# A four-stage ViT tower on one core: norm weight applied where the turned gelu rows leave the bank, projection in two terms, last stage written out in another order

## The chip, the core and the metric

The kernel runs on one NeuronCore of one Trainium2 chip. Its engines have queues of their own and meet through semaphores: TensorE (PE, matmuls, with weight loads shown as PEld), VectorE (DVE), ScalarE (ACT), GpSimd (POOL) and SyncE (SP), which here only issues DMAs. Each engine executes its list strictly in the order in which it is written, so an instruction that waits holds back all that stands behind it on its engine. The metric is the device time of one execution in microseconds (us); lower is better.

## The reference

32 images of 96x96 become 38 rows of 256 values each (36 patches, two tokens). Four blocks follow, each added to its input h: causal attention with rotary positions, a mixture of 8 linear experts, an attention with routed values and a small MLP, and a feed-forward part with ternary weights. The change is about the last:

```python
h = jnp.einsum('btd,hd->bth', x, absmean(W_fc))
h = jax.nn.gelu(h, approximate=False)
h = layernorm(h, ln_w, ln_b)
return jnp.einsum('bth,dh->btd', h, absmean(W_proj))
```

`absmean` makes each weight -1, 0 or 1. The hidden width is 1024. `ln_w` and `ln_b` hold one value for each hidden column.

## The kernel before

**Tiles and stages.** Three images make a tile of 114 rows (R), and there are 11 tiles (T). A tile passes stages a (first attention), c1 (experts), c2 and c3 (second attention and its MLP) and d (the last block). Stages overlap: while tile 7 is in c3, tile 10 may be in c1.

**What sets the order.** Every engine has an order written out by hand, as a list of small steps named by stage and tile, such as `c3_r1(9)` or `d2_proj(0)`. There are three loops: one over stage a; one, `c_step`, in which five tiles are in different parts of c1 to c3; and before the change one over the last stage, `d_step` (L2187 on PE), which runs for i from 4 to 10 with tile i - 3 in the projection and younger tiles in earlier steps. Between the first two loops lies a passage written out step by step (from `scores(7, True)`, L2198), and between the second and the third another (from `c2_x(9)`, L2294).

**Exact products.** A float32 value is split in a high and a low part, both in a narrower format that PE takes at full rate (fp32r). `mm3` (L1806) multiplies two such pairs with three matmuls: high by high, high by low, low by high.

**Stage d, tile by tile.** `d1_x` turns the normalised rows with PE; ACT and DVE take the high and low part out of the bank. `d1_fc` multiplies them by the ternary weights `fct`, four matmuls of 512 columns for each half of the hidden width. `d1_gelu` (ACT, L748) writes each half as 114x512 to `gel`; `d2_stats` (DVE, L1424) takes mean and variance of it. `d2_turn` (PE, L2175) turns the eight chunks of 128 columns into two banks, four chunks to a bank. `d2_hi` (ACT, L757) and `d2_lo` (DVE, L1438) write high and low part to `gth` and `gtl`, one instruction of 128x456 for each bank. `d2_proj` (PE, L2178) multiplies by the projection, eight chunks with `mm3`. `d2_centre` (DVE, L1446) subtracts the mean times the column sums `ncs`, `d2_out` (DVE, L1452) scales by 1/std and adds to h, and SP writes the tile out. Since mean and 1/std are applied behind the projection, the norm costs no pass over the hidden rows. There is one buffer each for `gel`, the banks of the turned rows, `gth`/`gtl`, and the projection's bank.

**The norm weight.** It is multiplied into the projection weights: ACT makes a high and a low version of the eight 128x256 chunks (`proj_hi` L726, `proj_lo` L734, 16 instructions), since the product with a float weight isn't ternary any more. `proj_sums` (L2141) sums them with 16 matmuls, `proj_bias` (L2134) adds `ln_b` through eight matmuls in float32, which the profile shows as 16.

Of the kernel before, what the change touches and what calls it, by code (L numbers as in the profile page):

```python
# [33 lines left out]
R = G * S  # L34
# [85 lines left out]
def vit_tower(nc, x_tiles, consts, vectors, rows, w_a, w_c, wqv, w_in, w_out, fc, proj, lnw, out):  # L120
    with ExitStack() as ctx:
# [3 lines left out]
        def sems(names):  # L125
# [42 lines left out]
        ones_r = sb("ones_r", [P, R], F32R)  # L168
# [11 lines left out]
        lnw_c = sb("lnw_c", [P, 2 * HC])  # L180
        lnwc_h = sb("lnwc_h", [P, HC], F32R)
# [13 lines left out]
        lnwc, lnwc_l = (lnw_c[:, i * HC:(i + 1) * HC] for i in range(2))  # L195
        lnbr = k_exp[:].rearrange("p f h r -> p (f h r)").rearrange("p (c r) -> p c r", c=HC)
        pw_h = ([wa[:, 0, HC * D + c * D:HC * D + (c + 1) * D] for c in range(6)]
                + [wa[:, 1, HC * D + c * D:HC * D + (c + 1) * D] for c in range(2)])
        pw_l = we_h[:, 1].rearrange("p e d -> p (e d)").rearrange("p (c n) -> p c n", c=HC)
# [36 lines left out]
        tern, tern_mm, fc_mm, gelu, g_stat, g_rstd, gT_mm, gT_hi, gT_lo, bw_ready, lnw_split, pw_ready, centred = sems(  # L236
            "tern tern_mm fc_mm gelu g_stat g_rstd gT_mm gT_hi gT_lo bw_ready lnw_split pw_ready centred")
# [23 lines left out]
        def _(sp):  # L261
# [42 lines left out]
            sp.dma_start(lnwc, lnw[0:1, :].rearrange("o (c p) -> p (o c)", p=P), allow_slow_non_contiguous=True).then_inc(lnw_in, 16)  # L304
# [9 lines left out]
        def _(gp):  # L314
# [109 lines left out]
            def d_step(i, first, last):  # L424
                on = [first <= k <= last for k in range(4)]
                if on[0]:
                    rstd(nD, i)
                if on[2]:
                    d2_rstd(i - 2)
                    d2_bias(i - 2)  # L430

# [9 lines left out]
            rstd(n1, 1)  # L441
            c1_add(0, (0, 1, 2, 3, 4, 5, 6, 7))
            rstd(n1, 2)
            rstd_pair(0)
            c1_add(1, (0,))
            rstd(n1, 3)
            c1_add(1, (1,))
            c2_keep(0)
            c1_add(1, (2, 3, 4, 5, 6, 7))
            rstd_pair(1)  # L450
            c1_add(2, (0, 1, 2, 3))
            c2_keep(1)
            c1_add(2, (4, 5))
            rstd(n1, 4)
            c1_add(2, (6, 7))
            c1_add(3, (0, 1))
            rstd_pair(2)
            c1_add(3, (2, 3, 4))
# [4 lines left out]
            c2_keep(2)  # L463
# [3 lines left out]
            c2_keep(9)  # L467
            rstd(nD, 0)
            c1_add(10, (0, 1, 2))
            rstd(n4, 7)  # L470
            c1_add(10, (3, 4))
            rstd(nD, 1)
            c1_add(10, (5, 6, 7))
            c3_bias(7)
            c3_h(7)
            rstd_pair(10)
            rstd(n4, 8)
            rstd(nD, 2)
            c3_bias(8)
            c3_h(8)  # L480
            rstd(n4, 9)
            c3_bias(9)
            d2_rstd(0)
            c3_h(9)
            c2_keep(10)
            rstd(n4, 10)
            c3_bias(10)
            d2_bias(0)
            rstd(nD, 3)
            d2_rstd(1)  # L490
            c3_h(10)
            d2_bias(1)
            with gp.Fori(4, T) as i:
                d_step(i, 0, 3)
            for i in range(T, T + 2):
                d_step(i, i - T + 1, 3)
# [3 lines left out]
        def _(act):  # L500
# [188 lines left out]
            def c_step(i):  # L689
# [20 lines left out]
                softmax_exp(i - 2 + T)  # L710
                c3_relu(i - 4, (0, 1, 2, 3))
                c2_pt(i - 2, (0,))
                c2_pt(i - 2, (1,))
                c1_gate(i)
                c2_pt(i - 2, (2, 3))

            def lnw_halves():
                act.activation(ones_r[:], ones[:, 0:R], ACT.Copy).then_inc(lnw_split, 1)
                act.wait_ge(lnw_in, 16)
                act.activation(lnwc_h[:], lnwc, ACT.Copy).then_inc(lnw_split, 1)  # L720

            def proj_hi(chunks):
                act.wait_ge(lnw_split, 3)
                act.wait_ge(tern, 8)
                for c in chunks:
# [1696 lines left out]
```

## Time and profile before

| | |
|---|---|
| time, median of 3 runs | 553.65 us (553.48 to 555.54) |
| the profiled execution, its own time | 550.58 us |
| its span | 548.8 us |
| PE busy | 506.9 us, 92% |
| PE weight loads | 426.6 us, 78% |
| DVE busy | 375.6 us, 68% |
| ACT busy | 272.9 us, 50% |
| POOL busy | 190.5 us, 35% |

Busy time is the time in which an engine has at least one instruction in progress. Two neighbours on DVE or ACT overlap a little in the profile, and matmuls overlap a lot, so the distance from start to start, not the duration, says what one more instruction costs on a full engine. The profile's clock for PE reads 1.00 where the full 2.4 GHz was granted. L12 is line 12 of the kernel.

### The profile page before, as it was taken

The numbers are of one execution on the slowest core, as the hardware profiler recorded it, in microseconds if no ns is written. First come the engines' busy times: TensorE is split into PE (matmuls) and PEld (weight loads), VectorE is DVE, ScalarE is ACT, GpSimd is POOL, SyncE is SP. The second block draws the span as 40 slices with busy tenths as digits, with TensorE's granted clock in tenths as the row PEclk, the third lists the DMA queues.
The fourth block names the chain that finished last, engine by engine and source line by source line (L and its number), as shares of the span: only waits on it lengthen the run. The fifth ranks groups of instructions, "written<-read, shape, count | busy, mean of one in ns | idle before, by whom it ended". The sixth has DMA issues, their size and how long they took to land.

```text
span 548.8 us, 12145 instructions
## 1 busy us (share of the span) xinstructions
PE 506.9 (92%) x3902; PEld 426.6 (78%) x3902; DVE 375.6 (68%) x943; ACT 272.9 (50%) x634; POOL 190.5 (35%) x257
## 2 busy tenths in 40 slices
PE   8989999999998878989999999999999989889996
PEld 7878877887877656667778888888888768678885
DVE  4555466546537776565997877878878687668874
ACT  4120322223233363357667677677677886444331
POOL 3232132132234210565555354364363412132330
PEclk9899999999999998999999999999999999999999
DMA  8934432533415000000000000000000000000000
GB/s 301 380 112 155 153 129 85 169 103 102 153 29 176 1 2 1 1 0 2 1 1 2 1 0 0 0 0 0 0 0 1 1 1 1 1 10 26 17 17 24
DMA packets 10990, 29.62 MB, mean 54 GB/s; under 512 B 2192, under 2 KB 3408, under 8 KB 10704
## 3 DMA queue, kind: packets, MB, share of 16 engines
q1 hardware_dynamic: 10960, 29.23, 15.9%
q8 instruction: 17, 0.28, 0.2%
q14 instruction: 13, 0.11, 0.1%
HBM read 27.98 MB, written 1.25 MB: 53 GB/s over the span
## 4 chain that ended last, share of the span: by engine, by line
PE 42%; DVE 6%; issue 5%; ACT 3%; POOL 1%; DVEq 1%; POOLq 0%; ACTq 0%
PE score L2069 6%; PE tb L1808 3%; PE score L1873 3%; PE bz L2099 3%; PE tb L1810 3%; PE tb L1809 3%; PE bank L1810 3%; PE bank L1809 3%; PE bank L1808 3%; PE tb L1891 2%; PE bz L2081 2%; PE bz L1822 1%; PE bz L1808 1%; DVE we_h L1438 1%; PE tb L1822 1%
## 5 line engine op out<-in xcount | busy, mean ns | idle before, releaser
L383 POOL TENSOR_TENSOR h<-h,scaled 114x256 f32 (+1 forms) x88 | 69.1, 785 | 49.9 <-ACT scaled L686 43.3
L335 POOL TENSOR_TENSOR small<-small,half 114x1 f32<-114x1 f32 x44 | 25.8, 586 | 136.5 <-DVE small L969 136.5
L552 ACT ACTIVATE p_exp<-sc,cst 114x608 f32<-114x608 f32 x66 | 48.2, 795 | 25.6 <-DVE sc L1050 25.6
L1923 PE MATMUL bz<-ebuf 128*128 128x256 f32 x256 | 58.7, 382 | 0.0
L560 ACT ACTIVATE pt<-tb 114x456 f32<-114x456 f32 x66 | 34.6, 556 | 36.0 <-PE tb L1891 36.0
L1923 PEld LDWEIGHTS bz<-ebuf 128*128 128x128 f32 x256 | 47.7, 192 | 5.9
L1891 PE MATMUL tb<-cst,p_exp 114*114 114x114 f32 x352 | 44.0, 266 | 6.1 <-ACT pt L560 3.3
L2069 PE MATMUL score<-v,pt 114*114 114x137 f32 x352 | 48.9, 282 | 0.3 <-ACT o L653 0.3
L686 ACT ACTIVATE scaled<-bank,gl 114x256 f32<-114x256 f32 x88 | 39.0, 473 | 17.3 <-PE bank L1810 6.2
L1891 PEld LDWEIGHTS tb<-cst,p_exp 114*114 114x114 f32 x352 | 35.2, 134 | 15.1 <-ACT pt L560 6.7
L2069 PEld LDWEIGHTS score<-v,pt 114*114 114x114 f32 x352 | 44.1, 178 | 2.1 <-issue 0.4
L1873 PE MATMUL score<-k_exp,q_exp 64*114 64x152 f32 x528 | 40.6, 298 | 0.9 <-DVE k_exp L1264 0.8
L1873 PEld LDWEIGHTS score<-k_exp,q_exp 64*114 64x114 f32 x528 | 35.2, 175 | 7.0 <-issue 6.9
L1808 PE MATMUL bank<-we_h,xth 128*114 128x512 f32 x88 | 38.2, 434 | 0.1
L1809 PE MATMUL bank<-we_l,xth 128*114 128x512 f32 x88 | 35.0, 398 | 0.0
L1810 PE MATMUL bank<-we_h,xtl 128*114 128x512 f32 x88 | 34.9, 397 | 0.0
L346 POOL TENSOR_TENSOR o<-o 114x512 f32<-114x512 f32 x11 | 14.0, 1274 | 59.5 <-DVE o L1030 59.5
L653 ACT ACTIVATE o<-score 114x411 f32<-114x411 f32 (+1 forms) x66 | 31.2, 480 | 2.9 <-PE score L2069 2.0
L509 ACT ACTIVATE xth<-bank 128x228 fp32r<-128x228 f32 x33 | 11.8, 358 | 35.8 <-PE bank L1822 35.8
L1808 PE MATMUL tb<-wa,we_h 128*114 128x256 f32 x88 | 25.7, 292 | 2.5 <-DVE we_h L1438 2.1
L1044 DVE TENSOR_REDUCE smax<-score 114x16 f32<-114x608 f32 x22 | 17.3, 786 | 13.0 <-PE score L1873 12.9
L757 ACT ACTIVATE we_h<-score 128x456 fp32r<-128x456 f32 x22 | 11.1, 550 | 28.5 <-PE score L2175 28.5
(218 smaller groups left out, 1349.6 us busy)
## 6 DMA issues: line engine op xcount, KB each, us to landing
ebuf<-in_w_in SPq DMA_DIRECT2D x16, 512.0 KB, 4.3
ebuf<-in_w_out SPq DMA_DIRECT2D x16, 512.0 KB, 5.1
x_raw<-in_x_tiles SPq DMA_DIRECT2D x11, 342.0 KB, 3.0
out<-h SPq DMA_DIRECT2D x10, 114.0 KB
raw<-in_w_a SPq DMA_DIRECT2D x4, 256.0 KB, 4.7
ebuf<-in_fc SPq DMA_DIRECT2D x1, 1024.0 KB, 4.8
ebuf<-in_proj SPq DMA_DIRECT2D x1, 1024.0 KB, 6.9
raw<-in_w_a SPq DMA_DIRECT2D x2, 384.0 KB, 5.7
```

Source lines behind the costliest of these rows:

```text
L383: gp.tensor_tensor(h[0:R, t, :], h[0:R, t, :], scaled[0:R, e % 4, :], ALU.add).then_inc(moe_acc, 1)
L552: act.activation(p_exp[0:R, :, b * S:(b + 1) * S], sc[0:R], ACT.Exp, bias=cst[0:R, CB + b:CB + b + 1], scale=SCALE).then_inc(exps, 1)
L560: act.activation(pt[0:R, 4 * g:4 * g + 4, :], tb[g % 2][0:R, 0:4 * R].rearrange("p (h r) -> p h r", h=4), ACT.Copy).then_inc(pt_odd if g % ...
L653: act.activation(o1[0:R, h0:h0 + k, :], score[0:R, g % 2, 0:k * VE].rearrange("p (h d) -> p h d", h=k), ACT.Copy).then_inc(pv1_out, 1)
L686: act.activation(scaled[0:R, e % 4, :], bk[1 + e // 2 % 2][0:R, (e % 2) * D:(e % 2 + 1) * D], ACT.Copy, scale=gl[0:R, 7, e:e + 1]).then_in ...
L1808: pe.matmul(dst, lh, rh_, start=first, stop=False)
L1809: pe.matmul(dst, lh, rl_, start=False, stop=False)
L1810: return pe.matmul(dst, ll, rh_, start=False, stop=last)
L1873: last = pe.matmul(score[0:R, i, f * HQ * S:(f + 1) * HQ * S], q_exp[rows64, f].rearrange("p b x -> p (b x)")[:, b * R:(b + 1) * R], k_exp ...
L1891: last = pe.transpose(tb[g % 2][0:R, i * R:(i + 1) * R], p_exp[0:R, 4 * g + i, :], cst[0:R, CI:CI + R])
L1923: last = pe.matmul(bz[:, m * D:(m + 1) * D], ebuf[:, 0, c * D + m * P:c * D + (m + 1) * P], ebuf[:, 1, c * D:(c + 1) * D], start=(c == 0 a ...
L2069: last = pe.matmul(score[0:R, g % 2, i * VE:(i + 1) * VE], pt[0:R, place(h0 + i), :], v1[0:R, :], start=True, stop=True)
```

## The change

The norm weight no longer goes into the projection weights. ACT multiplies by it as it writes the high part of the turned rows (`scale=`, one value for each partition), and DVE computes bank times weight minus high part. A weight is one value for each partition only within one chunk of 128 hidden columns, so each bank now takes four instructions of 128x114 instead of one of 128x456, on both engines. The projection weights stay ternary and need no low part: `d2_proj` has two matmuls a chunk instead of three. The 16 weight instructions on ACT go; `weight_wide` (one DVE copy) and a `proj_sums` of eight float32 matmuls take the place of the former sums.

The loop over stage d is gone. All its steps are written out and mixed into the third stage's last tiles. The passage between the first two loops has a new order too; the loops over stages a and c are as they were. `d2_proj(t)` now waits for the centring of tile t - 1 rather than for its end, and `d2_centre(t)` waits for that end instead.

```diff
-        lnw_c = sb("lnw_c", [P, 2 * HC])
-        lnwc_h = sb("lnwc_h", [P, HC], F32R)
+        lnwc = sb("lnwc", [P, HC])
...
-        pw_h = ([wa[:, 0, HC * D + c * D:HC * D + (c + 1) * D] for c in range(6)]
...
-        pw_l = we_h[:, 1].rearrange("p e d -> p (e d)").rearrange("p (c n) -> p c n", c=HC)
+        lnwr = p_exp[:, 0:HC, :]
...
# ScalarE
-            def lnw_halves():
...
-            def proj_hi(chunks):
...
-                for c in chunks:
-                    act.activation(pw_h[c], projt[:, c, :].bitcast(F32), ACT.Copy,
-                                   scale=lnwc_h[:, c:c + 1].bitcast(F32)).then_inc(pw_ready, 1)
-
-            def proj_lo(chunks):
...
             def d1_gelu(t, halves=(0, 1)):
...
-                        since(act, g_stat, 4 * t)
+                        since(act, g_stat, 4 * t - 2)
...
             def d2_hi(t, halves=(0, 1)):
...
-                    act.activation(gth[:, 4 * q:4 * q + 4, :], score[:, q, 0:4 * R].rearrange("p (c r) -> p c r", c=4),
-                                   ACT.Copy).then_inc(gT_hi, 1)
+                    for c in range(4):
+                        k = 4 * q + c
+                        last = act.activation(gth[:, k, :], score[:, q, c * R:(c + 1) * R], ACT.Copy, scale=lnwc[:, k:k + 1])
+                    last.then_inc(gT_hi, 1)
...
# VectorE
+            def weight_wide():
+                dve.wait_ge(pt_mm, 8 * T)
+                dve.wait_ge(lnw_in, 16)
+                V.tensor_copy(lnwr, lnwc[:].unsqueeze(2).broadcast_to([P, HC, R])).then_inc(widened, 1)
...
             def d2_lo(t, halves=(0, 1)):
                 for q in halves:
                     dve.wait_ge(gT_hi, 2 * t + q + 1)
-                    V.tensor_tensor(gtl[:, 4 * q:4 * q + 4, :], score[:, q, 0:4 * R].rearrange("p (c r) -> p c r", c=4),
-                                    gth[:, 4 * q:4 * q + 4, :].bitcast(F32), ALU.subtract).then_inc(gT_lo, 1)
+                    for c in range(4):
+                        k = 4 * q + c
+                        last = V.scalar_tensor_tensor(gtl[:, k, :], score[:, q, c * R:(c + 1) * R], lnwc[:, k:k + 1],
+                                                      gth[:, k, :].bitcast(F32), ALU.mult, ALU.subtract)
+                    last.then_inc(gT_lo, 1)
...
             def d2_centre(t):
...
+                since(dve, done, t)
+                dve.wait_ge(g_stat, 4 * t + 4)
                 dve.wait_ge(proj_mm, t + 1)
...
# TensorE
             def proj_sums():
...
-                    pe.matmul(tb[0][0:R, 0:D], ones_r[:], pw_h[c], start=(c == 0), stop=False)
-                    last = pe.matmul(tb[0][0:R, 0:D], ones_r[:], pw_l[:, c, :], start=False, stop=(c == HC - 1))
+                    last = pe.matmul(tb[1][0:R, D:2 * D], lnwr[:, c, :], projt[:, c, :].bitcast(F32), start=(c == 0), stop=(c == HC - 1))
                 last.then_inc(tern_mm, 1)
...
             def d2_proj(t):
...
-                since(pe, done, t)
+                since(pe, centred, t)
                 for c in range(HC):
-                    last = mm3(tb[0][0:R, 0:D], gth[:, c, :], gtl[:, c, :], pw_h[c], pw_l[:, c, :], c == 0, c == HC - 1)
+                    pe.matmul(tb[0][0:R, 0:D], gth[:, c, :], projt[:, c, :], start=(c == 0), stop=False)
+                    last = pe.matmul(tb[0][0:R, 0:D], gtl[:, c, :], projt[:, c, :], start=False, stop=(c == HC - 1))
                 last.then_inc(proj_mm, 1)
...
# TensorE's list: the end of the third stage, and what replaces the loop
             c3_att(10)
+            d1_fc(4, (0, 1))
             c3_wf(10)
-            d2_proj(0)
+            d2_proj(3)
+            d2_turn(4, (0, 1))
...
             c3_r2(10)
-            with pe.Fori(4, T) as i:
-                d_step(i, 0, 3)
-            for i in range(T, T + 3):
-                d_step(i, i - T + 1, 3)
+            d2_turn(8, (0,))
+            d1_x(9)
+            d2_proj(7)
...
```

**PE, the passage from stage a to c.** These are the matmuls around the scores of tile 10, from the last one of tile 0's gate (`wc`) on; `score<-cmask` and `score<-k_exp` are the scores of tile 10, `we_h` and `we_l` the experts' weights. Before:

```order
L1810 MATMUL bank<-wc,xtl 114x8
L1868 MATMUL score<-cmask,idb 114x304 x2
L1873 MATMUL score<-k_exp,q_exp 114x152 x12
L1808 MATMUL bank<-we_h,xth 114x512
L1809 MATMUL bank<-we_l,xth 114x512
L1810 MATMUL bank<-we_h,xtl 114x512
```

Now:

```order
L1897 MATMUL bank<-wc,xtl 114x8
L1895 MATMUL bank<-we_h,xth 114x512
L1896 MATMUL bank<-we_l,xth 114x512
L1897 MATMUL bank<-we_h,xtl 114x512
L1895 MATMUL bank<-we_h,xth 114x512
L1896 MATMUL bank<-we_l,xth 114x512
L1897 MATMUL bank<-we_h,xtl 114x512
L1955 MATMUL score<-cmask,idb 114x304 x2
```

The first expert product of tile 0 (six matmuls) now stands ahead of the scores, whose bank has to be read by DVE first; before it stood behind them.

**ACT, stage d.** This is the body of the loop before, where `we_h<-score` is the high part, `ebuf<-bank` the gelu and `xth<-bank` the high part of the turned input:

```order
L948 ISA
L757 ACTIVATE we_h<-score 128x456
L754 REGISTER_ALU
L757 ACTIVATE we_h<-score 128x456
L744 ISA
L117 REGISTER_ALU
L748 ACTIVATE ebuf<-bank 114x512
L744 REGISTER_ALU
L748 ACTIVATE ebuf<-bank 114x512
L117 ISA
L509 ACTIVATE xth<-bank 128x228
```

Now, around the third stage's last tile (`attT`, `x_raw`):

```order
L736 ACTIVATE ebuf<-bank 114x512 x2
L748 ACTIVATE we_h<-score,lnwc 128x114 x8
L518 ACTIVATE attT<-bz 128x228
L736 ACTIVATE ebuf<-bank 114x512 x2
L518 ACTIVATE xth<-bank 128x228
L748 ACTIVATE we_h<-score,lnwc 128x114 x8
L736 ACTIVATE ebuf<-bank 114x512 x2
L528 ACTIVATE x_raw<-bz,vec 128x114 x2
L534 ACTIVATE xth<-x_raw 128x228
L518 ACTIVATE xth<-bank 128x228
L748 ACTIVATE we_h<-score,lnwc 128x114 x8
```

The last tile's steps of stage c3 stand between stage d's steps of tiles 3 to 6, where before they stood ahead of the loop.

**DVE, stage d.** `x<-scaled` is the centring, `we_h` the low part, `h<-x` the output. Before, in the loop:

```order
L974 TENSOR_SCALAR xn<-h,small 114x256
L1437 ISA
L1438 TENSOR_TENSOR we_h<-score,we_h 128x456
L1437 REGISTER_ALU
L1438 TENSOR_TENSOR we_h<-score,we_h 128x456
L1412 REGISTER_ALU
L960 ISA
L960 BN_STATS small<-h 114x6
```

Now, near the end:

```order
L957 BN_STATS small<-h 114x6
L1449 SCALAR_TENSOR_TENSOR x<-scaled,qvs,tb 114x256
L1438 SCALAR_TENSOR_TENSOR we_h<-score,lnwc,we_h 128x114 x8
L1427 BN_AGGR small<-small 114x2
L1455 SCALAR_TENSOR_TENSOR h<-x,qvs,h 114x256
L978 TENSOR_TENSOR xtl<-bank,xth 128x228
L962 BN_AGGR small<-small 114x2
```

The low part comes directly behind the centring of the tile before and ahead of its output, with eight instructions instead of two.

## Rows read from the trace of the kernel before

**Rows 1.** busy time by stretch: stretch, length, then busy us of PE, PEld, DVE, ACT, POOL

```profile
0.00:170.00 170.00, 157.68 (x1314) 134.83 (x1316) 91.21 (x184) 44.62 (x89) 45.95 (x58) 0.99 0.48 163
170.00:250.00 80.00, 66.84 (x618) 51.78 (x615) 53.26 (x141) 36.61 (x78) 28.61 (x37) 0.98 0.03 7
250.00:290.00 40.00, 37.78 (x269) 31.36 (x268) 33.32 (x81) 27.54 (x69) 20.89 (x23) 1.00 0.00 1
290.00:416.70 126.70, 126.70 (x898) 107.90 (x897) 102.18 (x297) 92.04 (x235) 58.90 (x84) 1.00 0.00 0
416.70:486.10 69.40, 61.60 (x410) 50.57 (x409) 48.75 (x130) 49.40 (x118) 21.01 (x31) 1.00 0.01 3
486.10:536.80 50.70, 49.65 (x354) 43.91 (x352) 42.31 (x105) 21.14 (x43) 13.88 (x23) 1.00 0.06 18
536.80:548.80 12.00, 6.68 (x56) 6.25 (x55) 4.57 (x10) 1.59 (x3) 1.25 (x2) 0.97 0.08 23
```

**Rows 2.** the same view, one turn of the last loop

```profile
504.00:510.06 6.06, 5.91 (x45) 5.21 (x44) 5.18 (x14) 2.44 (x5) 1.80 (x4) 1.00 0.07 19
```

**Rows 3.** groups by shape, of the projection; then PE's timeline; then a chain row

```profile
L1808 PE MATMUL tb<-wa,we_h 128*114 128x256 f32 x88 | 25.7, 292 | 2.5 <-DVE we_h L1438 2.1
507.14 0.28 PE L1810 MATMUL tb<-wa,we_h 128*114 128x256 f32 x1
507.25 0.28 PE L1808 MATMUL tb<-wa,we_h 128*114 128x256 f32 x1
...
462.82 3.46 PE tb L2138 x16
```

**Rows 4.** DVE: timeline of the low part, groups by shape, two neighbours in the timeline

```profile
505.60 1.16 DVE L1438 TENSOR_TENSOR we_h<-score,we_h 128x456 fp32r<-128x456 f32 x2
...
L1264 DVE SCALAR_TENSOR_TENSOR k_exp<-tb,vec,cst 128x456 f32<-128x456 f32 x22 | 14.2, 687 | 4.3 <-PE tb L1822 4.3
L1446 DVE SCALAR_TENSOR_TENSOR x<-scaled,qvs,tb 114x256 f32<-114x256 f32 x11 | 5.3, 479 | 7.1 <-PE tb L1810 7.1
L1399 DVE COPY k_exp<-vec 128x912 f32<-128x912 f32 x1 | 0.6, 619 | 0.0
...
463.73 0.29 DVE L1296 TENSOR_TENSOR mx<-mx,qvs 114x128 f32<-114x128 f32 x1
463.94 0.15 DVE L1433 TENSOR_TENSOR qvs<-small,cst 114x2 f32<-114x2 f32 x1
```

**Rows 5.** ACT's timeline, 450 to 512 us

```profile
461.61 0.90 ACT L726 ACTIVATE wa<-wa,lnwc_h 128x256 fp32r<-128x256 f32 x2
...
470.56 1.28 ACT L748 ACT_TABLE_LOAD   x1
...
482.89 1.09 ACT L675 ACTIVATE x_raw<-bz,vec 128x114 f32<-128x114 f32 x4 [0.70 <-PE bz L1822]
...
504.26 0.99 ACT L757 ACTIVATE we_h<-score 128x456 fp32r<-128x456 f32 x2 [2.97 <-PE score L2175]
```

**Rows 6.** 170 to 250 us: PE's waits, a stretch with PE's clock, PE's timeline of the scores

```profile
PE score L1868 <- DVE y L1069: 3.6, 3, 1.4
PE tb L1891 <- ACT p_exp L552: 2.5, 2, 1.7
...
210.00:220.00 10.00, 7.81 (x54) 6.19 (x53) 6.65 (x21) 3.58 (x7) 0.00 (x0) 0.83 0.00 0
...
198.64 1.82 PE L1873 MATMUL score<-k_exp,q_exp 64*114 64x152 f32 x24
...
212.42 2.41 PE L1873 MATMUL score<-k_exp,q_exp 64*114 64x152 f32 x24
```

**Rows 7.** DVE's timeline: last additions of the third stage, then the chain's last row

```profile
457.26 0.42 DVE L1326 TENSOR_TENSOR h<-bz,h 114x256 f32<-114x256 f32 x1 [0.35 <-PE bz L2099]
...
486.06 0.42 DVE L1326 TENSOR_TENSOR h<-bz,h 114x256 f32<-114x256 f32 x1 [3.44 <-PE bz L2099]
...
545.50 0.48 DVE h L1452
```

More of the change, by code:

```diff
@@ new lines, in _ @@
+            d1_norm(5)
+            d2_stats(2, (1,))
+            d0_stats(6)
+            mix(10, 11)
+            aggr(nD, 6)
+            d2_out(0)
+            d1_x(4)
+            d2_centre(1)
+            plus_eps(nD, 6)
+            d2_lo(2, (0,))
+            d2_aggr(2)
+            d2_lo(2, (1,))
+            d2_eps(2)
+            d1_norm(6)
+            d2_stats(3, (0,))
+            d0_stats(7)
+            c3_res(9)
+            d2_stats(3, (1,))
+            mix(10, 12)
+            d2_out(1)
@@ L1792, in _ @@
-            d2_stats(1, (1,))
-            d2_centre(0)
-            d2_aggr(1)
-            d2_eps(1)
-            d2_out(0)
-            c3_res(10)
-            with dve.Fori(4, T) as i:
-                d_step(i, 0, 3)
-            for i in range(T, T + 3):
-                d_step(i, i - T + 1, 3)
+            d2_aggr(4)
+            d2_lo(4, (0,))
+            d2_centre(3)
+            d2_lo(4, (1,))
+            d2_eps(4)
+            plus_eps(nD, 7)
+            d2_out(3)
+            d2_stats(5, (0,))
@@ new lines, in _ @@
+            d1_x(6)
+            c3_x(10)
+            d2_stats(5, (1,))
+            d1_norm(7)
+            d0_stats(8)
+            d2_centre(4)
+            d2_lo(5, (0, 1))
+            d2_aggr(5)
+            d2_out(4)
+            d1_x(7)
+            aggr(nD, 8)
+            plus_eps(nD, 8)
+            d2_eps(5)
+            d2_stats(6, (0, 1))
+            d1_norm(8)
+            d2_centre(5)
+            d2_lo(6, (0, 1))
+            d2_aggr(6)
+            d0_stats(9)
+            d2_out(5)
@@ new lines, in _ @@
+            d2_eps(6)
+            aggr(nD, 9)
+            d2_stats(7, (0,))
+            d1_x(8)
+            d2_centre(6)
+            plus_eps(nD, 9)
+            d2_stats(7, (1,))
+            d2_out(6)
+            d1_norm(9)
+            d2_aggr(7)
+            d2_lo(7, (0,))
+            d2_eps(7)
+            d2_lo(7, (1,))
+            d2_stats(8, (0,))
+            c3_res(10)
+            d0_stats(10)
+            aggr(nD, 10)
+            d2_stats(8, (1,))
+            d2_aggr(8)
+            d1_x(9)
@@ new lines, in _ @@
+            plus_eps(nD, 10)
+            d2_centre(7)
+            d2_lo(8, (0, 1))
+            d2_eps(8)
+            d2_out(7)
+            d1_norm(10)
+            d2_stats(9, (0, 1))
+            d2_centre(8)
+            d1_x(10)
+            d2_out(8)
+            d2_lo(9, (0,))
+            d2_aggr(9)
+            d2_lo(9, (1,))
+            d2_eps(9)
+            d2_stats(10, (0, 1))
+            d2_centre(9)
+            d2_lo(10, (0, 1))
+            d2_out(9)
+            d2_aggr(10)
@@ L1804, in _ @@
+            d2_eps(10)
+            d2_centre(10)
+            d2_out(10)
         @block.tensor
@@ L2216, in _ @@
             a1_x(10)
-            a1_v(9)
             scores(9, True)
@@ L2220, in _ @@
             a1_qk(10)
+            c1_x(0)
+            a1_v(10)
             a1_turn(9, (0, 1, 2, 3))
-            a1_v(10)
-            c1_x(0)
             a1_qT(10)
```

821 lines of the change are left out of this document (430 added, 391 removed).

## The prediction, made before the changed kernel ran

> **What bounds the kernel now.** I read the busy shares first, then the busy time stretch by stretch, and last the timelines inside the stretches that the change touches. PE is busy 506.9 of 548.8 us, so 41.9 us of its idle time are all that a better order can win; the rest needs less work for PE. The stretches show where the idle time lies [rows 1]: 12.3 us before 170 us, 13.2 between 170 and 250 (the passage from stage a to stage c), 2.2 up to 290, none at all in the long c loop, 7.8 where the third stage runs out (416.7 to 486.1), 1.0 in the d loop and 5.3 at the end. The c loop is bound by PE alone, and the change leaves it alone; so does it the first 170 us. Everything is decided from 170 to 290 and from 416.7 on, where DVE starts its first instruction after the c loop.
>
> In the d loop a turn takes 6.06 us, of which PE is busy 5.91 and DVE 5.18 [rows 2]. PE bounds it, but DVE is only 0.88 us behind. That is the number to keep in mind.
>
> **PE's terms.** The projection of a tile has 24 matmuls now and 16 after. They start 0.11 to 0.12 us apart [rows 3]; 24 of them and the drain make half a turn, so I take 0.118. 88 matmuls go (one of the three groups of 88, all alike [rows 3]): 88 x 0.118 = 10.4 us. The sums of the columns lose 16 such matmuls, 1.9 us, and gain eight float32 ones of the form that the chain shows for the bias, 3.46 us [rows 3]. Net PE loses 10.4 + 1.9 - 3.5 = 8.8 us. Its busy time from 416.7 us on falls from 61.6 + 49.65 + 6.68 = 117.9 [rows 1] to 109.1 us.
>
> **DVE's terms.** The low part is two instructions of 456 columns, 1.16 us together, 1.08 from start to next start [rows 4]. Eight of 114 columns with a scalar from memory take its place, a form that the trace doesn't have. The same operation takes 687 ns at 456 columns and 479 at 256 [rows 4], a slope of 1.04 ns a column, so about 330 ns at 114. But DVE overlaps neighbours: one of 128 columns lasts 0.29 us and the next starts 0.21 behind it [rows 4]. Taking 0.07 to 0.08 off gives 0.25 us each, 2.0 a tile. The bounds are 0.19 (it costs no more than the slope from 128 plain columns) and 0.33 (no overlap): 1.5 to 2.6 a tile. I take 0.25, since the overlap shows wherever two independent instructions meet: +0.9 a tile, 9.9 for 11 tiles. The wide copy of the weight has the bias's form, 0.6 us [rows 4]. DVE from 416.7 on: 48.75 + 42.31 + 4.57 = 95.6 [rows 1], after 106.1 us.
>
> The Trainium skill's page "Perfetto Trace Analysis" (Optimizing Scalar/DVE Operations) speaks against the change: every DVE instruction on PSUM pays about 125 ns on top of its columns, every ScalarE one about 51 ns, and grouping helps when the engine is saturated. By it 66 more instructions cost DVE 8.3 us and ACT 3.4. For DVE that agrees with my 9.9; for ACT the rows say more, as follows.
>
> **ACT's terms.** Four instructions of 128x114 from a bank take 1.09 us [rows 5], the two of 456 columns 0.99. Eight are 7 x 0.246 + 0.353 = 2.07 us, so +1.08 a tile, 11.9 in all. The 16 weight instructions go at 0.45 each (two in 0.90 [rows 5]): -7.2. The program now switches between exp and gelu tables five times behind the first load instead of three, at 1.28 [rows 5]: +2.6. ACT from 416.7 on goes from 72.1 [rows 1] to about 79.4 of some 125 us. It has room; a price of nothing holds as long as DVE and PE have other tiles to work on while it writes the high part. Without that cover the whole 11.9 would be on the path.
>
> **Smaller things.** POOL has the same work, 36 us in the last three stretches together [rows 1]; but its list has the bias additions of tiles 0 and 1 ahead of `c3_h(9)`, and they wait for the new sums. I cost it at nothing, as DVE's addition of that tile stands far behind. SP's writes follow `done` as before. PE's relaxed wait (centring instead of output) takes 0.48 us out of the ring of each tile; with DVE full this buys nothing. The loop's register work on the queues goes, some tenths of a us a turn, all on engines that the next sums cover.
>
> **Two loads instead of one.** From 416.7 on, PE has 109.1 and DVE 106.1 us of work. Before, the two had 117.9 and 95.6 over the 129.3 us up to the last output, which ends at 545.98 [rows 7]: PE 91%, DVE 74%. So what limits is how densely DVE can be filled. The best that long stretches show is 81% in the c loop (102.18 of 126.7), 83% in 250 to 290 [rows 1] and 85.5% in the d loop [rows 2]. In the first 70 us of the tail it was at 70%, since the third stage's last tiles run one after another: the additions of tiles 8 and 10 are 28.8 us apart [rows 7], while PE waits. The new order puts stage d's tiles 0 to 6 into this. I take 85.5%: 106.1 / 0.855 = 124.1 us, which leaves PE at 88%. A second way to it: PE's 109.1, plus the end's idle. There the single buffers make a ring: high part 2.07, hop 0.1, low part of the second bank 1.07, projection (3.28 from low part to centring before, less 8 x 0.118) 2.34, together 5.6 us a tile, of which PE has 4.8 to do at most and in the last tile 2; with gelu and turning, some 7 us idle at the end, 4 that remain of the 7.8 in the third stage, and 3 for collisions with a full DVE: 123. The last output then ends 124.1 us after 416.7, at 540.8 instead of 545.98: 5.2 us earlier, of PE's 8.8.
>
> **The passage from a to c.** PE waits 3.6 us for DVE ahead of scores and 2.5 for ACT's exp ahead of the turning [rows 6]. The new order puts `c1_x(0)` and `a1_v(10)` in front of the one and an expert product of tile 0 in front of the other, about 1 and 1.4 us of work in holes of 1.7 and 1.4. In 210 to 220 us the granted clock is 0.83, behind such holes, and the scores take 2.41 instead of 1.82 us [rows 6]; with the six matmuls behind them at the lower of the two levels that is about 1.7 us, which full holes might save. Against it: DVE is at 83% from 250 on and the same work has to pass it. Between 0 and 6, I take 3 us.
>
> **Sum.** Span 548.8 - 5.2 - 3 = 540.6. The profiled execution adds 1.8 around its span (550.58): 542.4. The median of the runs lies 3.1 above the profiled execution (553.65), which I carry over: 545.5 us, 1.5% faster.
>
> **Rivals.**
> A. The order fills better than anything in the trace: DVE 90% (117.9 us, PE 92.5%) and 6 us from the passage. 545.5 - 6.2 - 3 = 536.3. For it: PE reached 100% in the c loop with DVE at 81%. Against it: two full engines leave no slack for either.
> B. DVE's small instructions overlap little, 0.32 each: 5.7 us more work, 111.8 / 0.855 = 130.8, and the time is 545.5 + 6.7 = 552.2: no change. For it: the low part reads what ACT has just written, and writes what PE waits for. Against it: the two low halves overlap today by 0.08.
> C. Slower: DVE becomes the engine that everything queues on, with holes of its own, because in one strict list the third stage's last steps stand behind low parts that wait for ACT's longer high part (2.07 instead of 0.99), and the low parts behind them in turn. At 78% the tail takes 136.0 us: 545.5 + 11.9 = 557.4. The turning point: the gain is gone when the tail takes 132.3 us, DVE at 80.2%. For it: 70% and 74% are what the tail had. Against it: most of those holes were there because PE was full or tile 10 alone was left.
> That the change does not do what it says is no rival: the order shows 16 matmuls in each of the 11 projections.
>
> **Chances.** Forecast 0.55, A 0.18, B 0.14, C 0.13. A measurement tells 0.5% from no change, 550.9 to 556.4. The forecast and A are faster but for 0.02, B lies on the edge (0.04 faster, 0.10 same), C is slower: 0.75 faster, 0.12 same, 0.13 slower. The range, 536 to 556, takes in A's time and B's, and leaves out most of C. The likeliest case alone is 541 to 550.
>
> **What would show it.** PE busy in all near 498; projections with 16 matmuls 0.118 apart; DVE's busy time some 10 us up, its eight low parts in about 2.0 us; ACT's eight high parts in about 2.1; the last addition of the third stage 25 to 35 us later than 486.06, about 20 before the end; no idle PE for over 1.5 us between 416 and 510; fewer waits of PE in 170 to 250 and no drop of the clock at 210. It is wrong if DVE's share in the tail is under 80%, if the eight low parts take over 2.5 us, or if PE stands for several us behind the third stage's last steps.

## The result, and the profile after

| | before | after |
|---|---|---|
| median (lowest to highest) | 553.66 us (553.48 to 555.54) | 544.36 us (543.21 to 545.03) |
| the profiled execution, its span | 550.58, 548.8 us | 544.11, 542.3 us |
| PE, DVE, ACT busy | 506.9, 375.6, 272.9 us | 498.7, 380.1, 280.1 us |

The ratio is 0.9832 (95% interval 0.981 to 0.9855), 9.3 us less. The forecast was 545.5, so it came within 1.2 us, but errors in opposite directions stand behind that. Beside the experiments the kernel before had medians of 552.59 to 553.14 us, so absolute times of different rounds are comparable to about 1 us only.

The busy time by stretch of the changed kernel, in the columns of [rows 1]: stretch, length, then PE, PEld, DVE, ACT, POOL. The cut at 419.20 is the same point of the work as 416.70 before, right behind the last addition of the c loop.

```profile
PE 498.7 (92%) x3814; PEld 418.8 (77%) x3814; DVE 380.1 (70%) x1009; ACT 280.1 (52%) x684; POOL 194.8 (36%) x257
...
0.00:170.00 170.00, 158.22 (x1308) 135.13 (x1310) 90.78 (x183) 44.56 (x89) 45.91 (x58) 0.99 0.47 161
170.00:250.00 80.00, 65.23 (x610) 50.93 (x610) 51.68 (x144) 35.09 (x74) 28.24 (x37) 0.98 0.04 9
250.00:290.00 40.00, 37.40 (x265) 30.91 (x265) 34.52 (x77) 28.14 (x68) 25.12 (x23) 1.00 0.00 1
290.00:419.20 129.20, 129.20 (x911) 109.98 (x910) 104.42 (x302) 93.56 (x240) 58.88 (x84) 1.00 0.00 0
419.20:542.30 123.10, 108.68 (x727) 91.89 (x725) 98.75 (x309) 78.74 (x216) 36.60 (x56) 0.97 0.04 11
```

From here on "the tail" is the time from the start of the c loop's last addition (DVE `h<-bz`, at 416.31 before and 418.83 after) to the start of the last output (545.50 [rows 7] and 538.99): 129.2 us before, 120.2 after. So the tail is 9.0 us shorter, and everything ahead of it 2.5 longer; the span is 6.5 shorter. In the tail PE has 9.2 us less to do (117.9 [rows 1] to 108.7) and stands idle as long as before: 129.3 less 117.9 was 11.4, and 539.5 less 419.2 less 108.7 is 11.6.

The low parts and their neighbours, in DVE's timeline: start, length, line, operation. The first six rows answer to [rows 4], the last five are the last tile.

```profile
515.07 1.01 DVE L1438 SCALAR_TENSOR_TENSOR we_h<-score,lnwc,we_h 128x114 fp32r<-128x114 f32 x4
516.00 0.14 DVE L1431 TENSOR_TENSOR qvs<-small,cst 114x2 f32<-114x2 f32 x1
516.07 1.05 DVE L1438 SCALAR_TENSOR_TENSOR we_h<-score,lnwc,we_h 128x114 fp32r<-128x114 f32 x4
517.05 0.68 DVE L1422 BATCH_NORM_STATS2 small<-ebuf 114x6 f32<-114x512 f32 x1
517.65 0.40 DVE L1323 TENSOR_TENSOR h<-bz,h 114x256 f32<-114x256 f32 x1
518.20 0.43 DVE L957 BATCH_NORM_STATS2 small<-h 114x6 f32<-114x256 f32 x1 [0.16 <-DVE h L1323]
...
533.11 2.05 DVE L1438 SCALAR_TENSOR_TENSOR we_h<-score,lnwc,we_h 128x114 fp32r<-128x114 f32 x8 [0.94 <-ACT we_h L748]
535.08 0.47 DVE L1455 SCALAR_TENSOR_TENSOR h<-x,qvs,h 114x256 f32<-114x256 f32 x1
535.48 0.20 DVE L1427 BATCH_NORM_AGGREGATE small<-small 114x2 f32<-114x12 f32 x1
535.71 0.16 DVE L1431 TENSOR_TENSOR qvs<-small,cst 114x2 f32<-114x2 f32 x1
538.48 0.48 DVE L1449 SCALAR_TENSOR_TENSOR x<-scaled,qvs,tb 114x256 f32<-114x256 f32 x1 [2.61 <-PE tb L2274]
```

Eight low parts take 2.05 us. The third stage's last addition is at 517.65. In the last tile PE starts its projection only behind all eight low parts. The groups by shape: count, busy time and mean ns of one, then the idle time in front and its releasers.

```profile
L2273 PE MATMUL tb<-wa,we_h 128*114 128x256 f32 x88 | 23.2, 299 | 6.2 <-DVE we_h L1438 6.2
L748 ACT ACTIVATE we_h<-score,lnwc 128x114 fp32r<-128x114 f32 x88 | 23.0, 373 | 15.1 <-PE score L2263 9.2 <-PE tb L2274 5.9
L1438 DVE SCALAR_TENSOR_TENSOR we_h<-score,lnwc,we_h 128x114 fp32r<-128x114 f32 x88 | 22.7, 324 | 3.8 <-ACT we_h L748 3.8
L1455 DVE SCALAR_TENSOR_TENSOR h<-x,qvs,h 114x256 f32<-114x256 f32 x11 | 5.2, 468 | 0.0
```

PE waits 6.2 us for low parts, ACT's high part 5.9 us for projections: each stands behind the other through the single buffer. In this last tile the clock fell as well: the projection's matmuls start 0.12 us apart up to 535.90 and 0.21 from there on.

### The profile page after: what moved, and what is told of

It is laid out like the page before. It is cut to its first block and busy times, and to the rows that moved or that the text cites. A ratio compares the mean times of both kernels' runs of the same rounds, so it can differ in the third digit from the quotient of the medians.

```text
span 542.3 us, 11847 instructions
## 1 busy us (share of the span) xinstructions
PE 498.7 (92%) x3814; PEld 418.8 (77%) x3814; DVE 380.1 (70%) x1009; ACT 280.1 (52%) x684; POOL 194.8 (36%) x257
## 5 line engine op out<-in xcount | busy, mean ns | idle before, releaser
L330 POOL TENSOR_TENSOR small<-small,half 114x1 f32<-114x1 f32 x44 | 28.6, 650 | 135.8 <-DVE small L966 135.8
L1960 PE MATMUL score<-k_exp,q_exp 64*114 64x152 f32 x528 | 41.7, 304 | 1.3 <-DVE k_exp L1261 1.3
L748 ACT ACTIVATE we_h<-score,lnwc 128x114 fp32r<-128x114 f32 x88 | 23.0, 373 | 15.1 <-PE score L2263 9.2
L2273 PE MATMUL tb<-wa,we_h 128*114 128x256 f32 x88 | 23.2, 299 | 6.2 <-DVE we_h L1438 6.2
```

The lines of the kernel that those rows point to most:

```text
L1960: last = pe.matmul(score[0:R, i, f * HQ * S:(f + 1) * HQ * S], q_exp[rows64, f].rearrange("p b x -> p (b x)")[:, b * R:(b + 1) * R], k_exp ...
L2273: pe.matmul(tb[0][0:R, 0:D], gth[:, c, :], projt[:, c, :], start=(c == 0), stop=False)
```

## The experiments

All ratios are to the kernel before, with 95% intervals. "Old passage" is the order of before between the loops over stages a and c, on all engines.

The tails below come from one profiled execution each, and in some of them the last tile's projection ran partly at the lower clock. The time from its first matmul's start to its last one's shows it: 1.83 to 1.87 us at the full clock for 16 matmuls, 2.80 for 24 as in before. The last column takes the excess off.

| kernel | tail, us | last projection, us | tail at the full clock |
|---|---|---|---|
| before | 129.2 | 2.80 | 129.2 |
| the changed kernel | 120.2 | 2.70 | 119.3 |
| old passage, twice | 120.5, 119.4 | 3.07, 1.85 | 119.2, 119.4 |
| one spot | 119.2 | 1.87 | 119.2 |
| third term (24 matmuls) | 131.1 | 5.05 | 128.8 |
| low whole, parts whole | 116.8, 111.9 | 3.16, 1.87 | 115.5, 111.9 |
| half waits, half ring | 114.1, 113.0 | 2.27, 1.83 | 113.7, 113.0 |

The four executions with the changed kernel's own tail agree within 0.2 us in the last column, and there the change is worth 9.9 us of tail.

**The passage alone, both ways.** The first kernel is the changed one with the old passage, the second is the kernel before with the new one. In PE's list:

```diff
             c1_gate(0)
-            c1_moe(0, (0,))
             scores(10, True)
-            c1_x(1)
-            c1_moe(0, (1,))
+            c1_moe(0, (0,))
             a2_wo(9)
```

> The changed kernel with the former order of the passage from stage a to stage c; arithmetic and tail as changed. Theory 1 (the new passage costs time by itself: in the changed kernel every mark from the first scores of c2 on came 2.0 to 2.9 us later, and the tail was 9.0 us shorter): the marks come back by 2.5 us, the span is 539.8 instead of 542.3 and the ratio to the kernel before about 0.979. Rival (the 2.5 us are where the clock happened to drop, not the order): no difference to the changed kernel, 542.3 and 0.983.

> The kernel before with the new order of the passage alone. Theory 1: 2.5 us longer, a span near 551.3, ratio 1.004, since the c loop behind the passage is full of work for PE and gives nothing back. Rival: same as before, ratio 1.000.

Measured: with the old passage 541.34 us, 0.9786 (0.9722 to 0.9851), its last c-loop addition at 416.02 and its tail 120.5 us; a second measurement gave 542.27, 0.9819 (0.9784 to 0.9854), 416.30 and 119.4. The kernel before with the new passage: 554.06, 1.0029 (1.0001 to 1.0058), its addition at 417.46. With the old passage the interval overlaps that of the changed kernel, so whole executions don't tell the two passages apart clearly; the marks below do. The tail's gain doesn't depend on the passage: it is all in the other parts of the change.

The tail of before with the new passage is 133.0 us, 3.8 longer than that of before, though nothing was edited there. PE waits for ACT as before ahead of the third stage's last product, but this product and what surrounds it ran at the lower clock. First before, then the new passage in before, then its busy time from 482 to 492 us:

```profile
484.04 1.98 PE L2099 MATMUL bz<-wr,x_raw 128*114 128x256 f32 x8 [1.19 <-ACT x_raw L675]
...
486.05 3.76 PE L2104 MATMUL bz<-wr,x_raw 128*114 128x256 f32 x8 [1.19 <-ACT x_raw L674]
...
482.00:492.00 10.00, 8.13 (x26) 5.74 (x26) 3.20 (x10) 2.79 (x7) 2.59 (x4) 0.50 0.05 13
```

So the old order of the tail, with tile 10 alone at this point, can lose 3.8 us to the clock. The profiled execution of before didn't. None of the executions with the written-out order shows a drop in the tail ahead of the last tile.

The absolute start times mix in how long the first 170 us took, which has nothing to do with the passage. DVE's maximum of tile 7's scores, ahead of the passage, starts at 171.27 in before and 171.72 in after. From it to the c loop's last addition:

| order of the passage | granted clock | kernels | us |
|---|---|---|---|
| old | full | old passage twice, two terms, half ring | 244.45 to 244.73 |
| old | 0.83 in 210 to 220 | before, before with half waits | 245.04, 245.06 |
| old | 0.83 in 200 to 220 | half waits | 247.48 |
| new | full | new passage in before | 245.48 |
| new | 0.83 in 240 to 250 or 230 to 240 | after, third term, low whole, parts whole | 247.08 to 247.39 |
| new, one spot as before | full | one spot | 246.25 |

At the full clock the order itself costs 0.9 us; that rests on one execution with the new order. A drop of the clock costs 1.6 more in the changed kernel. Four of the five executions with the new order had a drop and three of the seven with the old one, so that the order brings it about is likely but not shown. Together the changed kernel's passage took 2.1 us of the 2.5; 0.45 were lost ahead of it.

**One spot of the new passage.** In the changed kernel six small gate matmuls stand between the turning of tile 0's q and k and its scores. Before, an expert product of 1.7 us stood there. PE's timeline of the changed kernel, with its wait in brackets:

```profile
239.64 0.61 PE L1909 MATMUL tb<-cst,raw 114*128 114x114 f32 x4 [0.69 <-ACT raw L635]
240.02 0.24 PE L1895 MATMUL bank<-wc,xth 128*114 128x8 f32 x1
...
241.73 2.73 PE L1960 MATMUL score<-k_exp,q_exp 64*114 64x152 f32 x24 [0.97 <-DVE k_exp L1261]
244.39 0.77 PE L1895 MATMUL bank<-we_h,xth 128*114 128x512 f32 x1
```

The edit, with ACT's and DVE's steps `c1_x(2)` and the gate of tile 2 put behind q and k accordingly:

```diff
-            c1_moe(1, (2, 3))
+            c1_moe(1, (2,))
             c2_qk(0)
             c2_qT(0)
             c2_kT(0)
-            c1_gate(2)
+            c1_moe(1, (3,))
             c2_scores(0)
+            c1_gate(2)
```

> The changed kernel with one spot of its new passage put back as before: between turning tile 0's q and k and its scores in c2, PE has the last expert product of tile 1 again (six matmuls, 1.7 us), and the gate of tile 2 (six small ones) stands behind the scores; ACT and DVE follow (second input part and gate of tile 2 behind k and q of tile 0). All the rest of the new passage stays. Theory 1: nearly all of the passage's loss arises here. In the changed kernel PE waits 0.97 us for k_exp ahead of these scores, and they then run at the lower clock (2.73 us instead of 1.82), while with the old passage the product covers the wait. Then the maximum of tile 0's scores starts at 242.7 to 243.2 instead of 244.50, the wait for k_exp and the clock drop in 240 to 250 are gone, the last addition of the c loop starts near 417.2 instead of 418.83, and the ratio is about 0.980. Theory 2: the loss builds up along the passage (moved gate sums, stage a's last tiles), and a hole filled here opens one step on: the maximum may start earlier, but the c loop's last addition stays at 418.3 to 419 and the ratio at 0.983.

Measured: 544.55 us, 0.9842 (0.9805 to 0.988). PE's timeline there:

```profile
237.86 0.49 PE L1895 MATMUL tb<-wc,xth 128*114 128x512 f32 x1 [0.77 <-DVE xtl L982]
...
240.20 0.61 PE L1909 MATMUL tb<-cst,raw 114*128 114x114 f32 x4 [0.69 <-ACT raw L635]
240.58 0.46 PE L1895 MATMUL bank<-we_h,xth 128*114 128x512 f32 x1
...
242.29 1.82 PE L1960 MATMUL score<-k_exp,q_exp 64*114 64x152 f32 x24
```

The wait and the slow scores are gone as theory 1 said, but a wait of 0.77 us opened in front of the product of q and k, and later steps lost again 0.4 of what was left: tile 0's maximum starts 1.3 us earlier, counted from the mark, the c loop ends 0.9 earlier. From mark to mark it takes 246.25 us, 1.6 more than the old order. The total shows no gain. Theory 2 holds in the main: holes move from spot to spot, and no single one carries the loss.

**The arithmetic alone.** The kernel before, its orders and its loop, with weight and two terms as in the change, and with the change's waits (`d2_proj` for the centring, `d2_centre` for the end).

```diff
-                    last = mm3(tb[0][0:R, 0:D], gth[:, c, :], gtl[:, c, :], pw_h[c], pw_l[:, c, :], c == 0, c == HC - 1)
+                    pe.matmul(tb[0][0:R, 0:D], gth[:, c, :], projt[:, c, :], start=(c == 0), stop=False)
+                    last = pe.matmul(tb[0][0:R, 0:D], gtl[:, c, :], projt[:, c, :], start=False, stop=(c == HC - 1))
```

> The kernel before with the new arithmetic only (weight applied in eight small instructions on ACT and on DVE, two matmuls a chunk, new column sums) and with the former order, the d loop with it. Theory 1 (the saved matmuls become time only because the new order keeps PE supplied): in the d loop PE has 5.0 us a turn, but DVE 5.18 + 0.9 of work plus the 0.88 in which it waits, so a turn takes 6.1 to 6.9 us instead of 6.06; seven turns lose up to 6 us, the third stage wins 7 us of ACT's work that nobody waited for; ratio 0.998 to 1.010. Rival (the saved matmuls are the gain, wherever they stand): turns of 5.3 us, ratio 0.985.

Measured: 562.11 us, 1.0169 (1.0091 to 1.0248), slower than the 0.998 to 1.010 expected. Its tail is 142.2 us, 13 more than before. One turn of its last loop, in the columns of [rows 2], then two neighbouring instructions:

```profile
522.03:528.97 6.94, 5.25 (x35) 4.25 (x35) 6.27 (x20) 3.42 (x11) 1.80 (x3) 1.00 0.06 17
...
524.96 0.47 DVE L1416 SCALAR_TENSOR_TENSOR x<-scaled,qvs,tb 114x256 f32<-114x256 f32 x1
525.63 1.00 DVE L1422 SCALAR_TENSOR_TENSOR h<-x,qvs,h 114x256 f32 x1 [0.20 <-DVE x L1416]
...
528.96 0.38 PE L2157 MATMUL tb<-wa,we_h 128*114 128x256 f32 x1 [1.48 <-DVE we_h L1405]
```

The turn is 0.88 us longer [rows 2]. DVE is busy for 6.27 of 6.94 us and what is left are its own gaps between dependent neighbours, as the 0.20 above; PE waits 1.48. DVE has become the bound of the loop. PE's projections wait 15.1 us in ten tiles for low parts. Not all of the 13 us are the loop's: the six turns between outputs account for 5.2, and 4.2 arise just ahead, between the outputs of tiles 0 and 1 (14.56 us, where before took 10.40), where the granted clock was 0.53 from 481 to 491. This is the drop told above, and before's profiled execution was spared it. Even so the arithmetic alone is slower: the fastest of its four executions took 560.81 us, the slowest of before 556.81. Of the turn's 0.88 us, 0.3 come from the output instruction, which lasts 1.00 instead of 0.70 us because GpSimd runs beside it (last section).

**One more matmul a chunk.** The changed kernel with the low product done twice, so that PE gets its 88 matmuls back and all else stays.

```diff
+                    pe.matmul(tb[0][0:R, 0:D], gtl[:, c, :], projt[:, c, :], start=False, stop=False)
```

> The changed kernel with a third matmul for each chunk of the projection, a repetition of the low one, so that the low part counts twice in the output: 88 matmuls more, 10.4 us of PE's work. Theory 1 (PE's idle time in the tail stays near 11.6 us whatever it is given, so its work is the time): 8 to 10.4 us longer than the changed kernel, ratio to before about 1.000. Rival (the tail is bound by DVE at 82% and its small instructions, PE has room): under 4 us longer, ratio under 0.990.

Measured: 553.55 us, 1.0018 (0.9986 to 1.005). The tail (cut at 419.20, 0.95 us ahead of this kernel's own addition's end) and DVE's main wait in it, for the projection:

```profile
419.20:554.10 134.90, 121.10 (x823) 104.32 (x821) 99.71 (x312) 79.47 (x217) 36.56 (x56) 0.97 0.04 10
...
DVE x L1449 <- PE tb L2275: 13.9, 9, 4.9
```

The tail is 10.9 us longer (131.1), 9.5 at the full clock, where 88 x 0.118 [rows 3] are 10.4: nearly all of the matmuls' time is on the path, and the whole gain of the change is gone.

**Fewer instructions, weight left out.** One instruction of 128x456 a bank again, first for the low part alone, then for both parts.

```diff
-                    for c in range(4):
-                        k = 4 * q + c
-                        last = V.scalar_tensor_tensor(gtl[:, k, :], score[:, q, c * R:(c + 1) * R], lnwc[:, k:k + 1],
-                                                      gth[:, k, :].bitcast(F32), ALU.mult, ALU.subtract)
-                    last.then_inc(gT_lo, 1)
+                    V.tensor_tensor(gtl[:, 4 * q:4 * q + 4, :], score[:, q, 0:4 * R].rearrange("p (c r) -> p c r", c=4),
+                                    gth[:, 4 * q:4 * q + 4, :].bitcast(F32), ALU.subtract).then_inc(gT_lo, 1)
```

> The changed kernel with the low part written by one 128x456 subtraction for each bank, as before; it leaves the norm weight out of the low part. DVE has 9.8 us less work in the tail, PE and ACT the same. Theory 1 (PE's work sets the tail, DVE is a cover that holds): the ring of each tile loses 0.5 us (the second bank's low part 0.6 instead of 1.03), which counts only where PE waits for a low part, some 5 places: 2 to 3 us shorter than the changed kernel's 542.3, ratio to before 0.978 to 0.980. Rival (DVE bounds the tail): 7 to 9 us shorter, ratio 0.968.

> As the one before, and the high part too by one 128x456 copy for each bank: the norm weight is left out of the gelu rows altogether. ACT has another 12 us less work. Theory 1: the high part of both banks takes 1.0 instead of 2.08 us, again only where PE has nothing else, another 3 to 4 us: span about 536, ratio 0.970 to 0.973. The small instructions then cost 6 us of the 22 that they take on DVE and ACT. Rival (each engine's work is on the path): 12 us or more from ACT alone, ratio below 0.960.

Measured: 539.78 us, 0.9777 (0.9731 to 0.9823), tail 116.8; and 535.65, 0.9693 (0.9645 to 0.9741), tail 111.9. These two kernels leave the weight out, so they price it but can't replace it. DVE's 7.8 us less of busy time (98.75 to 90.97) bring 3.4 us of tail, 3.8 at the full clock. ACT's 10.2 us (78.58 to 68.36) bring 4.9, or 3.6 at the full clock, though ACT is busy for only two thirds of the tail. PE has the same work in all three. So neither engine's load bounds the tail, but the chain high part, low part, projection of a tile does, with ACT's part of it as dear as DVE's.

**The same chain, shorter by waits alone.** The changed kernel with the old passage, in which PE waits bank by bank. Then "half ring": the projection also reports its first four chunks, and ACT's high part waits for those alone. The kernel to compare them with is the second measurement of the old passage (told above), whose expectation stands first.

```diff
             def d2_turn(t, halves=(0, 1)):
-                pe.wait_ge(gelu, 2 * t + 2)
-                since(pe, gT_lo, 2 * t)
                 for q in halves:
+                    pe.wait_ge(gelu, 2 * t + q + 1)
+                    if t > 0:
+                        pe.wait_ge(gT_lo, 2 * t - 1 + q)
...
             def d2_proj(t):
-                pe.wait_ge(gT_lo, 2 * t + 2)
                 for c in range(HC):
+                    if c % 4 == 0:
+                        pe.wait_ge(gT_lo, 2 * t + 1 + c // 4)
...
# half ring, on top
-                last.then_inc(proj_mm, 1)
+                    if c % 4 == 3:
+                        last.then_inc(proj_mm, 1)
...
-                    if q == 0:
-                        since(act, proj_mm, t)
+                    if t > 0:
+                        act.wait_ge(proj_mm, 2 * t - 1 + q)
```

> The changed kernel with the former passage once more, on the same chip as the next kernel: 539.8 us of span, ratio 0.979.

> The changed kernel with the former passage, and PE's waits in stage d by bank: the projection's first four chunks wait for the first bank's low part alone, the turning of a bank waits for its own half of the gelu and for that bank's low part of the tile before. PE waited 6.2 us in 5 places for the low part ahead of projections and 1.8 us ahead of turnings. Theory 1 (PE's waits in stage d are the end of the ring of single buffers): each of the 5 waits loses up to the low part of the second bank, 1.0 us, but the projection's second four chunks then wait; the tail is 3 to 5 us shorter than with the former passage alone, span 535 to 537, ratio 0.970 to 0.973. Rival (the ring turns at DVE's and ACT's pace, so PE starts earlier and ends at the same time): under 1 us.

> The kernel half_waits, and the projection signals after its first four chunks too, so that ACT writes the next tile's high part for the first bank while PE still reads the second. ACT still waited 4.8 us in 4 places for the projection in half_waits. Theory 1 (the ring of single buffers is what leaves PE idle at the end): up to 0.94 us in each of the last three or four turns, 2 to 3 us shorter than half_waits, ratio to before 0.965 to 0.967. Rival (after the first split the rest of the waits are slack of ACT that nobody pays for): no difference, 0.970.

> The kernel before, arithmetic and order untouched, with PE's waits in stage d by bank as in half_waits. Theory 1 (the split pays only where the high and low parts are long and PE's list has nothing else): in the d loop PE is busy 5.91 of 6.06 us, the last projection gains 0.5 us; ratio 0.997 to 1.000. Rival (the split is a gain of its own, the same as on the changed kernel): 4 to 6 us, ratio 0.990.

Measured: half waits 536.29 us, 0.9699 (0.9664 to 0.9734), tail 114.1; half ring 534.48, 0.9664 (0.9623 to 0.9704), tail 113.0; the kernel before with the split waits only 551.63, 0.9963 (0.9932 to 0.9995), tail 128.2. The waits of half ring's tail and its last tile:

```profile
PE tb L2270 <- DVE we_h L1436: 2.3, 2, 2.0
...
525.12 2.05 DVE L1436 SCALAR_TENSOR_TENSOR we_h<-score,lnwc,we_h 128x114 fp32r<-128x114 f32 x8 [0.94 <-ACT we_h L749]
...
528.58 0.48 DVE L1447 SCALAR_TENSOR_TENSOR x<-scaled,qvs,tb 114x256 f32<-114x256 f32 x1 [0.70 <-PE tb L2271]
...
L749 ACT ACTIVATE we_h<-score,lnwc 128x114 fp32r<-128x114 f32 x88 | 23.4, 370 | 9.8 <-PE score L2259 8.3 <-PE tb L2271 1.5
```

PE's wait for low parts falls from 6.2 to 2.3 us, ACT's for projections from 5.9 to 1.5. In the last tile the centring starts 3.46 us after the first low part, in the changed kernel 5.37 (538.48 less 533.11). About 1 us of that difference is the clock; in the second old passage, at the full clock, it was 4.38:

```profile
530.75 2.06 DVE L1436 SCALAR_TENSOR_TENSOR we_h<-score,lnwc,we_h 128x114 fp32r<-128x114 f32 x8 [0.95 <-ACT we_h L749]
...
535.13 0.48 DVE L1447 SCALAR_TENSOR_TENSOR x<-scaled,qvs,tb 114x256 f32<-114x256 f32 x1 [1.62 <-PE tb L2269]
```

No engine has less to compute, and the tail is 6.3 us shorter at the full clock: the wait for both banks at once was the price. Nearly all of it comes from PE's split waits (5.6 us, where 3 to 5 were expected). The projection's second report brought 0.7 us where 2 to 3 were expected, and the intervals of the two ratios overlap, so its worth is not shown. Half ring has the lowest time of all, 9.9 us under the changed kernel. The kernel before gains 1.0 us in its tail from the split; its low part is shorter and PE is nearly full in its loop, and which of the two keeps the gain small was not tried.

## Why the prediction was right, step by step

- **PE's terms**: right. 498.7 us busy in all (forecast 498), 108.7 in the tail (109.1).
- **The low part's price**: right, 2.03 to 2.06 us a tile (2.0), inside bounds of 1.5 to 2.6.
- **DVE's sum**: wrong. It forecast 106.1 us in the tail and got 98.75. The price was right, but the sum took the rest of DVE's busy time as fixed. Of the 7.4 us it missed, about 5.4 are overlap: independent neighbours now run into each other where a loop turn had dependent ones side by side. The durations of all instructions add up to 105.6 us in before's tail and 119.2 in after's, so the overlap grew by 10.4, and only 5.0 of that lie among the low parts, which the forecast had counted. Another 1.5 are the output instruction, 468 ns instead of 667 in the loop, since GpSimd no longer runs beside it.
- **ACT's terms**: right, 2.08 us a tile (2.07) and 78.7 us in the tail (79.4). That they lie beside other work was wrong: parts whole shows 3.6 us of them on the path, at the full clock. The 66 instructions that this kernel saves took 10.2 us of ACT. By the Trainium skill ("Perfetto Trace Analysis", Optimizing Scalar/DVE Operations; 51 ns each) the estimate is 3.4 us. The comparison isn't a clean one, since this kernel also drops the weight as an operand: in after's trace an activation of 128x114 out of a bank takes 264 ns without such an operand (`q_exp<-tb`) and 373 with it. For DVE the same estimate was 8.3, and low whole shows 7.8.
- **"Two loads instead of one"**: this step failed. It set the tail by DVE's share, 85.5% of 124.1 us, and so gave the change 5.2 of PE's 8.8 us. The tail took 120.3 with DVE at 82%, and PE kept its idle time of some 11.5 us: the gain was PE's whole term. Third term shows it from the other side, since there 88 matmuls cost 9.5 us at the full clock. What stands between PE and a full tail is the tile's chain over one buffer, as the second way to the sum had it (123), not the load of DVE.
- **Rival C**, DVE as the bound with slower time: did not come about in the change, but it is what the arithmetic alone does in the old order, 1.7% slower. With this arithmetic the written-out order (and what it does to the clock, some 4 us by the drop above) is worth 22 us of tail, 142.2 to 120.2. This case has no run of that order with the old arithmetic. The nearest is third term, with PE's old load and the small instructions: its tail is 128.8 us at the full clock, before's 129.2, so the order did no more there than pay for the small instructions.
- **The passage**: wrong in sign, -3 forecast, +2.1 measured. The step that failed is that PE's work put into two holes is time won; PE was busy for 65.2 us of 170 to 250, where it was 66.8 before. The clock drop at 210 did go, as forecast, and PE was busier there; but a drop came back at 240, and the product put into the first hole was missing from a later one.
- **The third stage's last addition**: 31.6 us later (25 to 35), 24.7 before the end (about 20). PE's longest wait between 416 and 510 was 1.4 us (none over 1.5).
- **From span to median**: 3.1 us were carried over from before. After's median lies 0.25 above its profiled execution. In before the profiled execution was merely a quick one: other executions of it beside the first experiments went from 549.46 to 556.81. They follow the clock. With a mean granted clock of 0.993, that of the profiled one, they took 549.98 to 552.06 us, with 0.987 or 0.988 they took 553.85 to 554.18. So the difference between the medians, 9.3 us, is larger than that between the profiled executions, 6.5. Part of it may be the drop that the old tail can have; which executions of before had it no trace shows.

In the span, then, the tail came out 3.8 us better than forecast, and the stretches ahead of it 5.5 worse; -6.5 instead of -8.2. That left the span 1.7 us above the forecast, and the offset carried over was 2.9 too large. That the forecast lies within 1.2 us of the measurement is therefore partly luck: three errors, of -3.8, +5.5 and -2.9 us.

## What to carry to other kernels

Where a tile passes several engines over single buffers, add up its chain before the loads of the engines, and look at every wait that asks for more than the next instruction needs: splitting them by bank, and one report, gave 7.8 us (542.27 to 534.48), nearly as much as the whole change, and 6.0 of them came from the split alone. PE work that goes turns into time only as long as the order keeps PE supplied; the same arithmetic in the old loop was slower. When the order changes, ask which neighbours will overlap and what another engine will run beside them. Take intervals from a mark ahead of the edited stretch, not from the start of the execution, and compare tails only at the same clock.

## What the runs showed of the hardware

- The same instruction, `h<-x` of 114x256 on DVE, takes longer where GpSimd's addition `h<-h,scaled` runs beside it, and then ends 0.28 us after GpSimd does. First before, with almost no overlap and with much; then two terms in the old order, in the loop and behind it:

```profile
491.87 0.74 POOL L422 TENSOR_TENSOR h<-h,scaled 114x256 f32 x1
492.53 0.48 DVE L1452 SCALAR_TENSOR_TENSOR h<-x,qvs,h 114x256 f32 x1 [0.21 <-DVE x L1446]
504.33 0.74 POOL L422 TENSOR_TENSOR h<-h,scaled 114x256 f32 x1
504.65 0.70 DVE L1452 SCALAR_TENSOR_TENSOR h<-x,qvs,h 114x256 f32 x1 [0.19 <-DVE x L1446]
...
525.61 0.74 POOL L417 TENSOR_TENSOR h<-h,scaled 114x256 f32 x1
525.63 1.00 DVE L1422 SCALAR_TENSOR_TENSOR h<-x,qvs,h 114x256 f32 x1 [0.20 <-DVE x L1416]
545.22 0.73 POOL L417 TENSOR_TENSOR h<-h,scaled 114x256 f32<-114x256 f32 x1
545.64 0.59 DVE L1422 SCALAR_TENSOR_TENSOR h<-x,qvs,h 114x256 f32<-114x256 f32 x1
```

  The loop is not the reason: the instruction at 492.53 belongs to it and is short, the one at 545.64 stands behind it and is long. In after none of the eleven meets this addition, and they last 0.43 to 0.48 us. No run moved GpSimd's addition alone, so this is read from the traces and not from an experiment.
- The first 170 us scatter between executions: the mark at 171.27 in before lay between 169.95 and 172.65 in thirteen profiled executions. From the maximum at 73.00 to it there are 98.3 us in before and 98.3 in after, so the scatter arises in the first 73 us.
- What a drop to the lower clock costs depends on where it falls. In the passage, 10 us at 0.83 cost 0.4 us in before (scores of 2.41 instead of 1.82 us [rows 6]) and 1.6 in after, nearly all of the 1.7 us of full clock that were missing (scores of 2.73 us and the slow matmuls behind them). Two such stretches cost 2.9 us in half waits. In the last tile's projection the whole loss is on the path: 16 matmuls took up to 3.16 us from first to last start instead of 1.85.
